# Five of ten shared-expert groups run ahead of the expert tiles instead of behind them, with their inputs loaded ahead, in a one-core transformer layer

## The reference, cut to what matters

```python
def _L0_tok_ref(X, W, b, class_token, pos_embed):      # 128 images, 64 patches of 28 x 28 x 3 -> 128 values
    tokens = jnp.einsum('bpi,hi->bph', patches, W) + b
    return jnp.concatenate([cls, tokens], axis=1) * pos_embed

def _L0_attn_ref(x, W_c):                              # causal window of 64, softmax, output head
    ...
    return jax.nn.sigmoid(jnp.einsum('bsf,fo->bso', concat_vec, W_c))

def _L0_ffn_ref(x, ...):
    h = layer_norm(x, ln_in_g, ln_in_b)
    gate = jax.nn.softmax((h @ router_w + router_b) / TEMP, axis=-1)
    vals, idx = jax.lax.top_k(gate, TOP_K)             # 2 of 16 experts
    comb = jnp.sum(jax.nn.one_hot(idx, E, dtype=h.dtype) * vals[..., None], axis=-2)
    eh = jax.nn.silu(jnp.einsum('bsd,edh->ebsh', h, ew1) + eb1[:, None, None, :])
    ey = jnp.einsum('ebsh,ehd->ebsd', eh, ew2) + eb2[:, None, None, :]
    mix = jnp.einsum('bse,ebsd->bsd', comb, ey)
    shared = (jax.nn.silu(h @ sw1 + sb1) @ sw2 + sb2) * SHARED_SCALE
    moe_out = mix + shared
    fh = layer_norm(moe_out, ff_ln_g, ff_ln_b)
    ff_out = jax.nn.silu(fh @ ff_w1 + ff_b1) @ ff_w2 + ff_b2
    return x + moe_out + ff_out

h = _L0_tok_ref(x, ...)
h = h + _L0_attn_ref(_layernorm(h), W_c)
h = h + _L0_ffn_ref(_layernorm(h), ...)                # 128 x 65 tokens of 128 values, float32
```

## Time and profile before

| what | value |
|---|---|
| median of 3 executions (lowest, highest) | 974.96 us (974.53, 979.73) |
| span of the profiled execution | 976.1 us |
| TensorE busy | 874.8 us, 90% |
| VectorE, ScalarE, GpSimd busy | 674.0, 595.7, 438.7 us |
| mean granted TensorE clock | 0.970 |
| DMA | 186.96 MB, mean 192 GB/s |
| stage 2, first transposition to last down matmul | 510.6 to 793.6 us |
| first dense matmul of stage 3 | 843.9 us |

### The profile page before, as it was taken

How to read it: one execution, slowest core, us unless ns; L and a number is a source line. 1 busy time by engine, 2 the same in 40 slices (tenths; PEclk the granted TensorE clock), 3 DMA queues, 4 the chain that set the end, 5 groups by cost and what they waited for, 6 DMA issues and landing times. The chain is left out here.

```text
span 976.1 us, 22396 instructions
## 1 busy us (share of the span) xinstructions
PE 874.8 (90%) x5920; PEld 794.8 (81%) x5920; DVE 674.0 (69%) x2257; ACT 595.7 (61%) x1064; POOL 438.7 (45%) x374
## 2 busy tenths in 40 slices
PE   2879999999999999998808999999999986899996
PEld 1768888888888888887708999999999975788886
DVE  7457778787878778886626777777777735566662
ACT  2546666767666666676705666666656644477664
POOL 6012355555555555553542556655555641122320
PEclk9989999999999999999958999999999997999999
DMA  9999999999888888542269888888888841223321
GB/s 225 213 205 209 222 238 241 242 241 235 223 225 224 230 218 225 152 147 76 90 188 281 240 251 248 248 248 253 247 244 234 231 147 33 68 74 105 109 85 44
DMA packets 193915, 186.96 MB, mean 192 GB/s; under 512 B 16413, under 2 KB 168314, under 8 KB 193626
## 3 DMA queue, kind: packets, MB, share of 16 engines
q1 hardware_dynamic: 182208, 165.71, 64.4%
q0 software_dynamic: 9376, 19.42, 6.0%
q10 hardware_dynamic: 2298, 1.46, 0.5%
HBM read 150.48 MB, written 36.04 MB: 191 GB/s over the span
## 5 line engine op out<-in xcount | busy, mean ns | idle before, releaser
L1413 PE MATMUL bank<-xf,wp 128*128 128x256 f32 x1280 | 310.8, 391 | 6.6 <-ACT xf L621 6.6
L1413 PEld LDWEIGHTS bank<-xf,wp 128*128 128x128 f32 x1280 | 235.7, 190 | 48.8 <-issue 5.5
L858 POOL TENSOR_TENSOR rstd<-var,neghalf 128x4 f32<-128x4 f32 (+2 forms) x51 | 88.5, 1736 | 339.1 <-DVE var L1011 144.3
L899 POOL DMA_INDIRECT y_tok<-region,dsti x160 | 161.7, 1011 | 134.8 <-DVE region L1237 102.1
L621 ACT ACTIVATE xf<-region 128x1024 f32<-128x1024 f32 x160 | 174.3, 1140 | 7.7 <-DVE region L929 7.7
L874 POOL DMA_INDIRECT z_rows<-z,posg x130 | 151.7, 1167 | 37.7 <-issue 37.7
L1600 PE MATMUL bank<-region 128*128 128x128 f32 x1280 | 155.8, 275 | 0.0
L1600 PEld LDWEIGHTS bank<-region 128*128 128x128 f32 x1280 | 149.9, 192 | 0.0
L779 ACT ACTIVATE region<-bank,cols 128x256 f32<-128x256 f32 x320 | 126.0, 475 | 23.1 <-PE bank L1589 22.3
L929 DVE COPY region<-region 32x1792 f32<-32x1792 f32 x96 | 104.6, 1090 | 51.3 <-ACT hT L641 27.1
L1589 PE MATMUL bank<-parts 128*128 128x256 f32 x960 | 135.2, 290 | 2.4 <-DVE parts L1256 1.5
(11 more groups left out here) (180 smaller groups left out, 1230.5 us busy)
## 6 DMA issues: line engine op xcount, KB each, us to landing
region<-in_x SPq DMA_DIRECT2D x384, 196.0 KB
region<-in_L_ffn_ew SPq DMA_DIRECT2D x160, 256.0 KB
region<-z_rows SPq DMA_DIRECT2D x80, 130.0 KB
region<-y_tok SPq DMA_DIRECT2D x16, 512.0 KB, 5.3
out<-region SPq DMA_DIRECT2D x65, 64.0 KB
ht_dram<-hT SPq DMA_DIRECT2D x16, 256.0 KB, 4.2
r_dram<-rr SPq DMA_DIRECT2D x16, 256.0 KB, 3.0
region<-ht_dram SPq DMA_DIRECT2D x16, 256.0 KB, 3.0
```

The source lines that it names most:

```text
L858: pool.tensor_tensor(dst, var, neghalf[:, 0:var.shape[1]], ALU.pow).then_inc(ready, 1)
L899: pool.indirect_dma_start(y_tok, bass.IndirectOffsetOnAxis(dsti[n % 2][:, i:i + 1], 0), yout[n % 2][:, i], None).then_inc(y_free[n % 2], 16)
L1413: ins = pe.matmul(out_cols, wp[:, s], cols_in, start=s == 0, stop=s == MAIN - 1)
```

## The change

EARLY becomes 12 and a new number, FILL = 7, stands where 7 stood before for the groups inside the routing. Groups 0 to 4 keep their places. On TensorE group 7's up matmuls come ahead of the ranks of the last routed group, groups 8 to 11 follow between the routing and the first expert tile, and the down matmuls of group 11 stand behind the first transposition of expert rows. Groups 12 to 16 stay behind stage 2, all together, with `t_z(0)` behind them.

Inputs: groups 0 to 11 are loaded each into its own piece of `r_res` (free until the residual is loaded in stage 2), groups 0 to 5 while stage 1 still has one half of the image buffer, 6 to 11 when it has none; only the last five use the two buffers `ht3`. Each load has its own semaphore. The parts of the shared inputs are laid out anew in `parts`, so that tile 0's weights can be split before the last shared group is done.

All 16 zeroings are issued by SP, and four row numbers are read with one read. The bias table is loaded ahead of the last stores of stage 1. The expert table's transposes use bank 5, the transposed rows bank 7. In stage 3 VectorE has a new order among the late groups, and GpSimd waits for nmr before it adds the residual. GpSimd's scatter of the last full group is split: its first tile goes ahead of the last rstd.

```diff
-EARLY = 7
+FILL, EARLY = 7, 12
+assert EARLY % 2 == 0 and EARLY + 4 == GROUPS
...
+        def ht_in(i):
+            w = sh_tiles(i) * P
+            return r_res[:, i * GTOK:i * GTOK + w] if i < EARLY else ht3[i % 2][:, 0:w]
...
+        def row_numbers(eng, src):
+            return nc.values_load_multi_w_load_instructions(src, engines=[eng.engine], min_val=0, max_val=ZROWS - EROWS)[1]
+
-        def zero_tails(eng, first):
+        def zero_tails(eng):
             eng.wait_ge(tail_ready, 1)
-            with eng.Fori(0, E // 8) as e:
-                rows = [eng.value_load(tail[0:1, bass.ds(e * 4 + (first + n), 1)], min_val=0, max_val=ZROWS - EROWS)
-                        for n in range(4)]
-                for row in rows:
+            for n in range(0, E, 4):
+                for row in row_numbers(eng, tail[0:1, n:n + 4]):
                     eng.dma_start(z_rows[bass.ds(row, EROWS)]..., zsrc).then_inc(tails_zeroed, 16)
...
SP:
-            load_ht(0)
-            load_ht(1)
+            for i in range(HT_LOW):          # 6
+                load_ht(i)
             one(stores, GROUPS - 3)
...
-            load_ht(2)
-            load_ht(3)
+            sp.wait_ge(xact_ready, units_before(GROUPS, 0))
+            for i in range(HT_LOW, EARLY):
+                load_ht(i)
             one(stores, GROUPS - 2)
-            load_ht(4)
-            load_ht(5)
-            load_ht(6)
+            sp.wait_ge(xunit_used, units_before(GROUPS, 0))
+            sp.dma_start(eb2_rows, eb2...).then_inc(eb2_loaded, 16)
             one(stores, GROUPS - 1)
             one(stores, GROUPS)
-            zero_tails(sp, 0)
+            zero_tails(sp)
...
-            rows = [first_row(j) for j in range(4)]
+            rows = row_numbers(sp, rowj[0:1, 0:4])
...
             expert_rows(0, 0, rows[0])
-            sp.dma_start(eb2_rows, eb2...).then_inc(eb2_loaded, 16)
...
ScalarE:
-            sh_silu(5)
-            sh_silu(6)
+            shared(5)
+            shared(6)
             one(take_z, GROUPS)
             one(take_r, GROUPS)
             exp_table()
             route_b(GROUPS)
-            zero_tails(act, E // 2)
+            for i in range(FILL, EARLY - 2):
+                shared(i)
+            sh_silu(EARLY - 2)
+            sh_silu(EARLY - 1)
...
GpSimd:
             groups(pool, 2, GROUPS, step)
+            scatter(GROUPS - 1, 1, 1)
             rstd(var2_ready, GROUPS + 1, ...)
-            scatter(GROUPS - 1, 1)
+            scatter(GROUPS - 1, 1, GT, 1)
...
                 rstd(var4_ready, q + 1, rstd1[:, :], var1[:, :], rstd4_ready)
+                pool.wait_ge(nmr_ready, q + 1)
                 res = ...
                 pool.tensor_tensor(res, res, moe[k][:, 0:nt], ALU.add).then_inc(res_ready, 1)
...
VectorE:
+                if not attn:
+                    ht_low(FILL)
                 dve.wait_ge(rstd2_ready, r + 1)
...
                     sh_rows(4)
+                    ht_low(FILL + 1)
...
-                if not attn:
-                    sh_rows(5)
...
+            sh_rows(FILL - 2)
             dve.wait_ge(tej_done, 1)
...
-            sh_rows(6)
             dve.wait_ge(tab_ready, 1)
+            for i in range(FILL, EARLY):
+                if i + 2 < EARLY:
+                    ht_low(i + 2)
+                sh_rows(i - 1)
...
+            split_w1(0, 0, 0)
+            dve.wait_ge(shu_done, SC * EARLY)
+            split_rows(0, 0)
+            sh_rows(EARLY - 1)
+            split_w1(1, 1, 0)
             dve.wait_ge(eb2_loaded, 16)
-            split_rows(0, 0)
-            split_w1(0, 0, 0)
-            split_w1(1, 1, 0)
...
TensorE:
             gates(GROUPS, 0)
-            sh_down(6)
+            sh_up(FILL)
             ranks(GROUPS)
+            sh_down(FILL - 1)
+            sh_up(FILL + 1)
...
+            for i in range(FILL + 2, EARLY):
+                sh_down(i - 2)
+                sh_up(i)
+            sh_down(EARLY - 2)
...
+            t_in(0, 0, 0)
+            sh_down(EARLY - 1)
             pe.wait_ge(shr_ready, EARLY)
-            t_in(0, 0, 0)
...
-            for i in range(EARLY, EARLY + 3):
-                sh_up(i)
-                if i > EARLY:
-                    sh_down(i - 1)
-            t_z(0)
-            for i in range(EARLY + 3, GROUPS + 1):
+            sh_up(EARLY)
+            for i in range(EARLY + 1, GROUPS + 1):
                 sh_up(i)
                 sh_down(i - 1)
             sh_down(GROUPS)
+            t_z(0)
```

More of the change, by code:

```diff
@@ L570, in _ @@
                 load_gat(q, q)
-            for i in range(EARLY + 4, GROUPS + 1):
-                load_ht(i)
             for q in range(2, 4):
@@ L823, in _ @@
             ht_high(EARLY + 1)
-            for i in range(EARLY, EARLY + 3):
-                shared(i)
-            z_norm(0, 0)
-            z_in(0)
-            for i in range(EARLY + 3, GROUPS - 1):
+            for i in range(EARLY, GROUPS - 1):
                 shared(i)
@@ L870, in scatter @@
                 plain(pool)
-                for t in range(nt):
+                for t in range(first, nt):
                     for s in range(TOPK):
@@ L1291, in _ @@
             fb2_rows(GROUPS, 1)
-            for j in range(EXPERT_TILES - 4, EXPERT_TILES + 1):
+            for j in range(EXPERT_TILES - 4, EXPERT_TILES):
                 step2(j, j)
+            dve.wait_ge(up_done, EXPERT_TILES * EC)
+            ht_low(EARLY)
+            ht_low(EARLY + 1)
+            step2(EXPERT_TILES, EXPERT_TILES)
             def add_rows(q, k, s, nt, done):
```

68 lines of the change are left out of this document (33 added, 35 removed).

## The result

The kernel after takes 949.65 us (median of 4 runs, 944.70 to 952.95), the kernel before, run beside it, 974.75 (4 runs, 971.85 to 979.73): ratio 0.9728, 95% interval 0.9698 to 0.9757. The forecast was 946.6 in a range of 942 to 953, faster with a chance of 0.97. The profiled execution of after took 951.7 us, its span is 949.8.

What follows compares the result with a forecast made beforehand. TensorE's pace was taken to bound the kernel outside two dents, where time could be won. Late gain 26.8 plus front 1.6 gave 28.4 us off the median 974.96: 946.6 us, range 942 to 953, the forecast's own range 944 to 949.

Steps and rivals of the forecast that it cites:

- The late gain: Between last expert matmul and last stage: five groups left, group 0's chain last; 26.8 us after 2.0 charged for the clock.
- rival E: Second dent: the late groups' own inputs are last, TensorE through only at 820, time 952 us; chance 0.05.
- The first step: First dense step of the last stage: TensorE at half clock after idling, longer dense matmuls; 2.0 us charged.
- The front: Five groups moved between routing and first expert tile, covered by the wait for rows: gain 1.6 us, bounds -1.9 to +4.6.
- SP's 16 zeroings: SP's queue after routing: 16 zeroings with joint number reads take 13.0 to 15.8 us, 0.8 to 3.6 later than before.
- the tiles after that keep their distance: Expert stage behind the first tile: later tiles follow at unchanged spacing, so the 1.6 us won at up(2) stays.
- The addition behind nmr: Last stage: GpSimd's residual addition waits for nmr; 1.07 us won in group 0's chain, 0 charged per step, bounds 0 and 1.0.
- only has to be done by then: Last stage's steps: VectorE waits 2.1 us each before h4_low, so up to 1.25 lost ahead of it fits in.
- B: Single queue makes rows 1.9 late; late gather, addition in group 0's chain or slower clock cost 2 to 4: 950-953; chance 0.18.
- A: TensorE stays awake in the first dent, front +4.5, and the clock costs 0.5 instead of 2 in the second: 942; chance 0.15.
- C: Last stage's steps: the addition beside the mix isn't covered, 1.0 a step, 15 us: 962; chance 0.04.
- D: Last stage's steps: the same addition costs VectorE over 4.0 us each, slower than before, 978 at 4.2 a step; chance 0.02.

Runs made afterwards that it cites:

- e2: Kernel after with one up term instead of three for shared groups 7 to 16, part of the computation left out: 951.09 us, ratio to before 0.973.
- f1: Kernel before with only the late groups' order changed, all ten shared groups ahead of group 0's transposition, nothing moved to the front: 968.41 us, ratio 0.989.
- e1: Kernel after, unchanged, run again as the base of its series: 948.61 us, ratio to before 0.969.
- e4: Kernel after without GpSimd's wait for nmr ahead of the residual addition: 946.72 us, ratio to before 0.969.
- f2: Kernel after, unchanged, run again as the measure for its neighbours: 950.43 us, ratio to before 0.972.
- f3: Kernel after with the second half of the zeroings on ScalarE's queue again: 949.38 us, ratio to before 0.970.
- f4: Kernel after with zeroing on two queues, tile 4's loads first, no wait for nmr, and 6 and 13 idle matmuls around t_z(0): 952.85 us, ratio 0.975.
- e7: Kernel after with 48 idle matmuls ahead of t_in(0), on a slower chip: 1033.90 us.
- e8: Kernel after with tile 4's rows and weights issued ahead of six loads for the last stage, on a slower chip: 1040.96 us.
- e6: Kernel after with 12 idle matmuls before and 28 after t_z(0), on a slower chip: 1042.87 us.

## Why the prediction was right, and where it was not

**The late gain, right in mechanism and size.** 28.8 was the term, 29.2 is the measure. The forecast put the mix of group 0 at 804.0 and had 11.1 from there to the dense matmuls; they are 803.78 and 11.07. TensorE was not last (e2): it was through at 809.1, not at 820, and rival E is out. Of the gain 9.5 are the order's (f1), which the prediction did not part from the rest.

**The first step, right in size and in cause as far as it was seen.** 2.0 was charged for the clock, 1.9 was lost in this execution, and 1.1 to 1.7 in e1, e4, f2 and f3; so the 2.0 is near the upper end of what the clock takes here. The first dense matmuls of after are 2.1 longer at half clock, and in all five executions the step follows their length. But there is a second limit, which the prediction took to be done in time: in f4, at full clock, 1.1 of the loss stays, for group 1's chain on VectorE and ScalarE. How much of that 1.1 would stay with the wait for nmr is open.

**The front, step by step.** SP's 16 zeroings: 15.5 us after tail, inside 13.0 to 15.8, near its upper end; the 13.0 had no room for the slow first load that the sentence names. The stretch of the row numbers took 1.7 less (508.68 - 506.99 = 1.69 instead of 508.42 - 504.99 = 3.43), inside 1.7 to 2.4, but that is luck. 0.9 of the 3.43 was SP waiting for the zeroings to land:

```profile
SPq L501 <- DMA z_rows<-zeros: 0.9, 1, 0.9
```

The forecast took the whole stretch for reading. Joint reading saved some 0.8, and the wait was gone: the last zeroing had landed 3.4 us after its issue, where in before SP waited until 5.9 after it. Why is not shown; in e2 and e4 SP waits 0.5 there. First rows 0.3 later (0.9 counted from tail), forecast no change. TensorE done at 504.6 (504.5), down 11 3.62 at half clock (3.4), up(0) at 516.0 at full clock (515.5). Up(2) came 0.86 earlier instead of 1.6, 0.75 lost in small pieces: rows 0.3, down 11 0.2, and the rest between up(0) and up(2). **The step that failed is "the tiles after that keep their distance":** tile 4's rows stand on SP behind six other loads, and were ready just in time only because TensorE was late. A fixed time on another queue took the 0.86 in this execution; in f2 it took 0.4, in e1 next to nothing, so over the executions the front gain is not lost at this place alone. It is small against the spread of the 300 us behind it (302.0 to 304.7), and no run shows it. The sum was 2.1 us too high, made up so: 2.4 by the front segment (0.8 longer instead of 1.6 shorter, counted from tail), 0.8 by the addition, below, and 1.1 taken back by a tail that came 0.6 earlier, a late segment 0.4 better and a first step 0.1 better. The tail varies by 5 us over the executions, so its 0.6 is chance.

**The addition behind nmr.** nmr fell from 1.23 to 0.16, as forecast, and the steps stayed at 7.7. VectorE's wait before h4_low shrank from 37.3 to 22.1 us over its 16 times (36.6 in e4) and did not vanish, so the cover in the steps held. Charged at 0, it costs 0.8 to 0.9 at the end of the kernel (14 profiles), and of the 1.07 that it was to win 0.65 is left at the first dense matmuls, where VectorE's order is last. The step that failed is that what precedes h4_low "only has to be done by then": the mix also releases the gather on SP, each gather releases the next mix, and the last out3 and its stores stand behind that. The Trainium skill (SBUF — State Buffer, Who interferes with whom) says that a VectorE instruction with two SBUF inputs and a GpSimd instruction that reads SBUF exclude each other; the traces agree on both sides, nmr 1.23 against 0.16 and half a mix 2.17 against 1.13. The wait moves the collision from one place to the other, and does not remove it.

**The rivals.** The 949.65 lies in the stated range, but just above the forecast's own 944 to 949 and just below B's 950 to 953. A (TensorE stays awake) needed the idle matmuls of e7 even to be seen. B's prices came, but small: rows 0.3 late instead of 1.9, and 0.8 from the addition, in the last steps and not in group 0's chain. C and D fell with steps of 7.7.

What stays open: whether the idle matmuls with the wait for nmr kept, and tile 4's rows (without its weights) issued first, would save 1 to 2 us (an estimate from the 1.1 to 1.9 of the first step and the 0 to 1.4 of tile 4's stall). Neither was tried. Why the expert stage varies by 3 us between executions of the same program, and what the front part alone is worth, is open too: no kernel had the front part without the late one.

## What to carry to other kernels

When work is moved into an idle stretch, ask what each engine does next on a fixed time: here a queue entry four tiles on took the small gain back in the profiled execution, while the large one, whose whole chain was worked out, came to within 0.4 us. A gain that is smaller than the spread of the stage behind it can't be shown by whole runs. Split a gain between "moved out" and "put in another order" with one kernel; a third of this one needed no move. A mend that takes a stall away has to be followed to the next instruction behind it in the same queue, since two of the four here, the second queue and tile 4's loads, only handed the stall on. And when a gap in a trace is taken for the cost of one thing, look first for a wait in it.

## What the runs showed of the hardware

- A shorter stop of TensorE did not give a shorter slow stretch. After 5.44, 6.18, 6.31, 6.66 and 6.76 us of idleness before t_in(0) half clock ended with down 11, which took 3.41 to 3.62 instead of 1.95 (e8, f2, after, e1, e4); after 3.99, 4.25 and 4.44 (f3, e6, f4), and after 10.38 (e2), up(0) was slow too, 2.91 instead of 1.67. What decides between them isn't shown.
- A matmul of 128 by 128 in f32 takes 0.23 us in a row of its kind at full clock (10.88 for 48, e7) and appears as two records of half that.
- Where one of these VectorE instructions meets GpSimd's residual addition, one or both take longer: nmr 1.23 to 1.25 instead of 0.16 (before, e4, f4), four mix instructions 2.17 instead of 1.13 with the addition at 1.46 instead of 1.25 (after), a 128x512 split 1.23 instead of 0.69 (f4).
- The last five output stores on SP's queue take 5.1 us to issue when the queue has stood for 2.4 us before them, 6.3 when it has stood for 1.3 (before, after).
- Two chips ran the same kernel in 978 and 1055 us. TensorE's undisturbed groups take the same (1.62 and 1.95) on both; the expert segment takes 337 to 346 instead of 302 to 305, and the same zeroing puts the first rows 23 to 25 us after tail instead of 19.
